# Waiting one round later for gathers to land, in the two convolutions of a graph network

## The reference, cut to what matters

```
def gine_conv(x, edge_index, w1, b1, w2, b2):
    src, dst = (edge_index[0], edge_index[1])
    msg = jax.nn.relu(x[src])
    agg = jax.ops.segment_sum(msg, dst, num_segments=x.shape[0])
    h = x + agg
    h = jax.nn.relu(h @ w1 + b1)
    return h @ w2 + b2
out = jax.nn.relu(gine_conv(x, edge_index, w11, b11, w12, b12))
out = gine_conv(out, edge_index, w21, b21, w22, b22)
```

## Time and profile before

| what | us |
|---|---|
| time, median of 3 runs (7104.03 to 7115.21) | 7106.12 |
| the profiled execution's own time | 7045.45 |
| its span, from the first to the last instruction | 7043.1 |
| POOL busy | 3563.8 |
| PE busy | 3443.0 |
| DVE busy | 2838.6 |
| ACT busy | 1926.4 |

### The profile page before, as it was taken

One profiled execution on the slowest core, in us unless ns is written; L12 is line 12 of the kernel. 1 busy time (PEld: TensorE's weight loads), 2 busy tenths in 40 slices (PEclk: granted clock), 3 DMA queues, 4 the chain that ended last, 5 costly groups with the idle time before them and its releaser, 6 DMA issues. The chain is left out here.

```text
span 7043.1 us, 79417 instructions
## 1 busy us (share of the span) xinstructions
PE 3443.0 (49%) x13479; PEld 2512.4 (36%) x13480; DVE 2838.6 (40%) x7047; ACT 1926.4 (27%) x4744; POOL 3563.8 (51%) x3729
## 2 busy tenths in 40 slices
PE   3445555445355555557423561244555552307990
PEld 0133333334244444446313451133434331204660
DVE  4644444422144444434422254444444446611222
ACT  0232222222233333332101210244444441112331
POOL 0066666666766666665676774455555551050005
PEclk9577777778777777778766786577777776558995
DMA  2232222223133333332101120011111111233113
GB/s 65 68 89 84 84 85 85 85 84 51 36 91 89 90 90 91 90 87 38 21 1 20 28 32 7 16 21 21 21 21 21 20 21 5 111 113 109 55 55 114
DMA packets 280599, 407.39 MB, mean 58 GB/s; under 512 B 93992, under 2 KB 197766, under 8 KB 280263
## 3 DMA queue, kind: packets, MB, share of 16 engines
q0 software_dynamic: 142720, 275.10, 16.6%
q1 hardware_dynamic: 137798, 131.50, 6.0%
HBM read 323.82 MB, written 81.61 MB: 58 GB/s over the span
## 5 line engine op out<-in xcount | busy, mean ns | idle before, releaser
L1070 PE MATMUL conv_ps<-conv_msg,conv_S 128*128 128x256 f32 x3328 | 1233.4, 549 | 1216.9 <-DMA conv_msg<-relu_xn_table,GI 659.2
L1070 PEld LDWEIGHTS conv_ps<-conv_msg,conv_S 128*128 128x128 f32 x3328 | 934.3, 290 | 1543.4 <-issue 1338.7
L1043 DVE TENSOR_TENSOR ACC<-ACC,conv_ps 128x256 f32 x1664 | 700.1, 421 | 1449.0 <-PE conv_ps L1070 1245.2
L994 POOL DMA_INDIRECT conv_msg<-relu_xn_table,GI x832 | 792.5, 953 | 702.7 <-DMA conv_msg<-relu_xn_table,GI 267.0
L1761 POOL DMA_INDIRECT gat_msg<-attn_table,GI x832 | 789.8, 949 | 602.9 <-DVE gat_M L1907 359.5
L994 POOL DMA_INDIRECT conv_msg<-conv_table,GI x832 | 786.8, 946 | 510.4 <-DMA conv_msg<-conv_table,GI 268.6
L1814 PE MATMUL gat_ps<-gat_M,gat_S 128*128 128x260 f32 x1664 | 645.1, 553 | 637.6 <-DVE gat_M L1907 601.6
L1014 ACT ACTIVATE conv_S<-iota_row,LOC 128x128 f32<-128x128 f32 x1664 | 507.9, 388 | 1019.0 <-PE conv_ps L1070 766.9
L1814 PEld LDWEIGHTS gat_ps<-gat_M,gat_S 128*128 128x128 f32 x1664 | 442.6, 281 | 748.6 <-issue 659.9
L1868 DVE TENSOR_TENSOR ACC<-ACC,gat_ps 128x260 f32 x832 | 351.9, 423 | 679.1 <-DMA conv_table<-mlp_a 427.7
L818 POOL DMA_INDIRECT edges_by_src<-mlp_lanes_pay,mlp_lanes_idx x288 | 342.7, 1190 | 109.7 <-issue 76.8
(11 more groups left out here) (388 smaller groups left out, 5171.4 us busy)
## 6 DMA issues: line engine op xcount, KB each, us to landing
expert_in<-router_zrow SPq DMA_DIRECT2D x53, 256.0 KB
experts_xe<-expert_in SPq DMA_DIRECT2D x106, 128.0 KB
expert_out<-experts_y SPq DMA_DIRECT2D x106, 128.0 KB
conv_msg<-relu_xn_table,GI POOLq DMA_INDIRECT x832
conv_msg<-conv_table,GI POOLq DMA_INDIRECT x832
gat_msg<-attn_table,GI POOLq DMA_INDIRECT x832
relu_xn_table<-norm_rx SPq DMA_DIRECT2D x49, 128.0 KB
xnT<-norm_xt SPq DMA_DIRECT2D x49, 128.0 KB
```

The costliest lines, as they stand in the source:

```text
L994: pool.indirect_dma_start(msg[:, h * RING + k, :], None, table, bass.IndirectOffsetOnAxis(ap=m.GI[:, t:t + 1], axis=0)).then_inc(got[h], 16)
L1043: nc.vector.tensor_tensor(acc, acc, ps[k % NB][:, 0:D], ALU.add).then_inc(added, 1)
L1070: nc.tensor.matmul(ps[k % NB][:, 0:D], S[:, h % 2, k, :], msg[:, h * RING + k, :], start=True, stop=True).then_inc(summed, 1)
```

## The change

The semaphore of each of the four sets of places becomes a pair, one for gathers 0 to 3 of a round and one for gathers 4 to 7. POOL no longer waits once per round for all gathers of the last round. It waits ahead of gather 0 for gathers 0 to 3 of the last round, and ahead of gather 4 for gathers 4 to 7 of the last round. PE waits for both semaphores of the pair before a round's sums. The wait for `summed` stays as it is.

```
-        NB, DEEP = 4, 4
+        NB, DEEP, HALF = 4, 4, RING // 2
-        got = st.sems("got", DEEP)
+        got = [st.sems(f"got{h}_", 2) for h in range(DEEP)]
         def landed(r, h):
-            return (r - h) * (16 * RING // DEEP) + 16 * RING
+            return (r - h) * (16 * HALF // DEEP) + 16 * HALF
         def _(pool):
...
                     pool.wait_ge(summed, (r - DEEP + 1) * RING)
-                if r >= 1:
-                    pool.wait_ge(got[(r - 1) % DEEP], ((r - 1) // DEEP + 1) * 16 * RING)
                 for k in range(RING):
                     t = r * RING + k
+                    if k % HALF == 0 and r >= 1:
+                        pool.wait_ge(got[(r - 1) % DEEP][k // HALF], ((r - 1) // DEEP + 1) * 16 * HALF)
                     pool.indirect_dma_start(msg[:, h * RING + k, :], None, table,
-                                            bass.IndirectOffsetOnAxis(ap=m.GI[:, t:t + 1], axis=0)).then_inc(got[h], 16)
+                                            bass.IndirectOffsetOnAxis(ap=m.GI[:, t:t + 1], axis=0)).then_inc(got[h][k // HALF], 16)
...
             def sums(r, h, chunk, keys):
-                pe.wait_ge(got[h], landed(r, h))
+                for half in range(2):
+                    pe.wait_ge(got[h][half], landed(r, h))
```

## The result

The changed kernel is slower: 7314.91 us median (7313.59 to 7317.74) against 7106.12, a ratio of 1.0291 (95% interval 1.0268 to 1.0315). The forecast was 6644, its range 6605 to 6740.

What follows compares the result with a forecast made beforehand. POOL's loop of eight gather issues and one landing was taken as the bound. The profiled 7045.45 us less 462.2 (479.5 saved, 17.3 kept by padding) gave 6583.2; plus 60.7, 6643.9 us, range 6605 to 6740.

Steps and rivals of the forecast that it cites:

- (a): POOL's landing waits in both convolutions: the half-round waits find their semaphore already there, gaining 479.5 of 541.3 us.
- (b): Padding rounds at each convolution's end: six waits keep 17.3 us as transfer time, leaving 462.2 us taken off.
- (c): Added semaphores and waits on POOL and PE: cost taken as 0, with bounds of 0 and 86 us.
- R1: Rival at POOL's rounds: each still pays for a second wait, 86 us in all, giving 6730 us; chance 0.11.
- (d): Instruction refills, 16 issue gaps of 1.88 us, 25 us in all: no change counted, 25 us kept for the range.
- (e): Other engines in the convolutions: none overtakes POOL's new round of 9.98 us; DVE nearest at 9.4, at most 10.2.
- R3: Rival at POOL's gathers: those in flight are limited elsewhere, so issue itself stalls, giving 7106 us; chance 0.03.
- R4: Rival at the transfers: no longer draining between rounds, they slow each other, 760 us more, 7866 us; chance 0.03.
- R2: Rival in the ranked rounds: DVE becomes the bound and 42 us come back, giving 6686 us; chance 0.07.
- The 60.7 us: Unexplained excess of the shown runs' median, 7106.12 us, over the profiled execution, added to the forecast unchanged.

Runs made afterwards that it cites:

- e3_split_drained: The changed kernel, but POOL waits for both halves of the last round at the round's start; 7065.32 us against 7053.89 for the kernel before, ratio 1.0016.
- e2_one_round_older: The kernel before, with single semaphores, but POOL waits ahead of a round for the landing of the round before the last; ratio to the kernel before 1.0216.
- the probe: Kernels computing nothing of the reference, only copying x, where engines signal beside rows of transfers; beside 1 KB gathers PE's release of itself went from 0.85 to 5.60 us.

## Why the prediction was wrong

**(a) The landing waits.** Right as far as it goes: both half-round waits find their semaphore, 541.3 us became 2.8. But what POOL saved was also the break that kept it under the service rate: 12.18 / 8 = 1.52 us a gather before, 1.25 after.

**(b) Padding.** I had six waits keep 17.3 us. The waits for a landing are gone, but the last sums of conv1 start 8.6 us behind the end of the last gather. My sign for this term, padding rounds above 13 us each, is met by some and not by others: the last three rounds of conv1 take 13.56, 10.02 and 13.14 us. The term is small and was not measured by itself.

**(c) Semaphores and waits at 0.** Right: 11 us by e3_split_drained, of the 86 allowed. R1 falls.

**(d) Refills.** The 16 gaps of 1.88 us are gone, most of the long gaps that are left have 0.53 to 0.60 us, and the longest is 1.4 where it was 2.9. That is inside the bound of 25 us. No run shows what the gaps are.

**(e) "None overtakes POOL."** This step failed. I added up the durations of DVE, PE and ACT between signals and took the signals' own delay from rounds that run at 1.52 us a gather. The durations held; PE's signals became 4 to 5 us late each, and a chain of eight sums and eight adds hangs on them. POOL then waits for `summed` of three rounds back, 6 us every second round.

**The rivals.** R3 ("limited elsewhere") was nearest and got 0.03, because I took the 32 gathers of the earlier trace rows as evidence that a long row is harmless. They were harmless to POOL's issue. The 14.41 us that POOL then waits for DVE stand in the earlier trace rows too, and I passed over them; they come right behind the late starts of DVE and ACT. The same window has PE at 3.12 of 40 us, and one more view, the timeline of the other engines, shows the stall that decided this case. R4 had the sign and not the mechanism: DMA stayed at 0.29 and landings in time. R2 came out at nothing: where the signals are quick, a ranked round of DVE takes 8.53 us (990.46 to 998.99 in e2_one_round_older), less than POOL's 9.98 and than my 9.4 to 10.2. The 60.7 us that I carried over without a reason are about the difference between the two lengths of the attention stage.

**What is shown and what is not.** Shown in the kernels: the loss comes with uninterrupted issue of gathers and goes with its pace, and PE's signals are what is late. Shown in the probe: PE's signals are late by far the most, those of DVE, ACT and POOL by less; the lateness does not depend on rows or bytes, and it is absent beside plain transfers. That a queue served at 1.40 us a gather is behind it is an inference from the common 67.3 us. By it alone the start of the trouble is not explained: at the first late turn of DVE and ACT the gathers issued are 4.7 us behind such a queue with 16 rows (18 gathers, 1.14 us apart), 3.3 us with 128 (22, 1.25) and 1.2 us at 1.36 us apart (30). What is served there, and why PE's signals suffer most, is open. The Trainium skill (GPSIMD Engine Reference, section When to use GPSIMD) says that a pair of GpSimd's cores generates the descriptors of such transfers and rings the doorbells; no run here isolates those writes, and plain transfers by POOL, which by that sentence need them too, were harmless at 0.54 us each. The real kernel's border lies higher than the probe's (POOL still waits 114.5 us for PE at 1.44 us a gather, never at 1.52); that the engines' own signals take the difference is argued, from conv2 against conv1, not shown. Nor is it shown that all of these 114.5 us are the same trouble.

## What to carry to other kernels

Before taking away a wait that looks idle, ask at what rate the engine behind it will then run, and look in the profile for a place that already runs at that rate, at all engines and not only at the one that is sped up. In long rows of gathers less than about 1.4 us apart the other engines' signals began to be late here, TensorE's above all, and a short useless instruction between gathers can make the whole faster. A wait whose two sides have both long been done is the mark of it in a trace.

## What the runs showed of the hardware

- GpSimd issued 48 gathers in a row 1.25 us apart (1.14 with 16 rows), and its own rows never show that anything is behind: each is 0.94 or 0.95 us, the first 1.09.
- In such a row a turn of VectorE and ScalarE, two signals, takes 1.40 us (0.60 in quiet), a turn of TensorE by itself 5.60 (0.85). Most late turns are near multiples of 0.70 us: 1.40, 2.10, 3.50, 4.20, 4.90, 5.60.
- The backlog outlives the row: after the last gather (98.0 us) it took 8.5 us until the signals were quick again.
- A drain of GpSimd right behind a gather and a memset holds the next instruction 1.97 us; the memset itself starts with the gather's end (1004.87).
- Plain transfers from GpSimd (119 GB/s) or SyncE (117 GB/s), 48 in a row, delay no signal: 126 passes of TensorE in 53 and 54 us, where it makes 52 in 59 us beside gathers.
